# One transformer block in FP32 on one core: values get a buffer of their own, and the order of the stages is rewritten

## The reference

```python
x = x + attn_block(layernorm(x))     # pre-norm, LINEAR attention over the 16 heads of EACH token, MLP 256-1024-256
x = x + moe(layernorm(x))            # 8 experts, gates from the mean over the 2048 tokens of a batch

# attn_block, per token n (H=16 heads, HD=16):
fq, fk = elu(q) + 1, elu(k) + 1
kv = einsum('bhnd,bhne->bnde', fk, v);  qkv = einsum('bhnd,bnde->bhne', fq, kv)
attn = qkv / (einsum('bhnd,bnd->bhn', fq, fk.sum(1))[..., None] + 1e-6)
x = q_x + attn @ wo + bo
return x + (gelu(ln(x) @ fc_w + fc_b) @ proj_w + proj_b)

# moe: softmax over the logits that reach the second largest (normally 2 experts)
out = sum_e gates[b, e] * gelu(x @ expert_w[e].T + expert_b[e])
```

## Time and profile before

| | us |
|---|---|
| median of 3 runs | 1278.87 |
| the profiled execution | 1278.0 |
| its span on the core | 1276.2 |
| PE busy | 1108.7 (87% of the span) |
| DVE busy | 782.9 (61%) |
| ACT busy | 530.4 (42%) |
| POOL busy | 190.8 (15%) |
| one step, 9 to 10 (from the transposes of `X` to the next ones) | 68.55 |

### The profile page before, as it was taken

How to read it: one execution, slowest core, us unless ns; L and a number is a source line. 1 busy time by engine, 2 the same in 40 slices (tenths; PEclk the granted TensorE clock), 3 DMA queues, 4 the chain that set the end, 5 groups by cost and what they waited for, 6 DMA issues and landing times.

```text
span 1276.2 us, 22032 instructions
## 1 busy us (share of the span) xinstructions
PE 1108.7 (87%) x7272; PEld 816.2 (64%) x7272; DVE 782.9 (61%) x1692; ACT 530.4 (42%) x835; POOL 190.8 (15%) x113
## 2 busy tenths in 40 slices
PE   6646988979797989999997989999999989795946
PEld 3444766757575858686775758586767667583723
DVE  2465566565757586666756676766666674646333
ACT  2413443534444444536353454536363444231322
POOL 1011202020111212120301112121203012111000
PEclk9757897979797989989897989899897989797969
DMA  4966656383737475665737473656658374311013
GB/s 161 187 143 157 116 140 149 104 180 95 173 98 173 104 165 115 173 148 153 168 121 173 114 172 116 160 128 173 148 147 174 125 165 106 102 55 53 17 66 116
DMA packets 242518, 170.21 MB, mean 133 GB/s; under 512 B 177040, under 2 KB 218256, under 8 KB 240144
## 3 DMA queue, kind: packets, MB, share of 16 engines
q1 hardware_dynamic: 235792, 158.80, 52.3%
q10 hardware_dynamic: 6656, 10.50, 2.4%
HBM read 93.75 MB, written 75.50 MB: 133 GB/s over the span
## 4 chain that ended last, share of the span: by engine, by line
PE 48%; issue 23%; DVE 14%; ACT 7%; DMA 3%; SPq 2%; POOL 1%; DVEq 1%; ACTq 0%; POOLq 0%
PE pq L963 13%; PE pj L949 10%; PE ps L925 7%; PE pq L869 5%; PE pt L934 4%; PE pt L857 3%; DVE nd L727 2%; DVE acc L818 2%; DVE am L700 1%; DVE hn L631 1%; ACT am L513 1%; DVE stat L621 1%; DMA scratch_nd<-ot 1%; DMA ot<-scratch_v 1%; SPq L366 1%
## 5 line engine op out<-in xcount | busy, mean ns | idle before, releaser
L716 DVE TENSOR_TENSOR hidden<-xhT,hidden 128x512 fp32r<-128x512 f32 x128 | 96.6, 755 | 224.0 <-ACT hidden L541 224.0
L963 PE MATMUL pq<-hT,w_fc 128*128 128x512 f32 x768 | 225.4, 433 | 9.4 <-DVE hT L723 5.2
L540 ACT ACTIVATE xhT<-pq,col 128x512 f32<-128x512 f32 x128 | 88.0, 688 | 323.1 <-PE pq L963 322.9
L949 PE MATMUL pj<-w_pj,hidden 128*128 128x256 f32 x1536 | 214.1, 288 | 0.7 <-DVE hidden L716 0.7
L949 PEld LDWEIGHTS pj<-w_pj,hidden 128*128 128x128 f32 x1536 | 191.6, 189 | 18.6 <-issue 9.8
L925 PE MATMUL ps<-kq 48*128 48x128 f32 x1024 | 155.7, 436 | 24.0 <-DVE am L700 14.7
L963 PEld LDWEIGHTS pq<-hT,w_fc 128*128 128x128 f32 x768 | 149.0, 207 | 41.3 <-issue 7.7
L700 DVE TENSOR_TENSOR am<-ps,mask 128x512 f32<-128x512 f32 x256 | 164.1, 682 | 17.4 <-PE ps L925 17.1
L925 PEld LDWEIGHTS ps<-kq 48*128 48x128 f32 x1024 | 133.8, 329 | 61.1 <-issue 36.9
L869 PE MATMUL pq<-zT,w_e 128*128 (+1 forms) x256 | 119.4, 614 | 11.8 <-DMA b_e<-in_eb 7.3
L458 POOL TENSOR_TENSOR rs<-var,mhalf 128x4 f32<-128x4 f32 x16 | 18.1, 1132 | 571.2 <-DVE var L744 571.2
(11 more groups left out here) (117 smaller groups left out, 1399.3 us busy)
## 6 DMA issues: line engine op xcount, KB each, us to landing
kq<-scratch_q SPq DMA_DIRECT2D x192, 128.0 KB, 3.7
kq<-scratch_k SPq DMA_DIRECT2D x192, 128.0 KB, 4.5
scratch_q<-hidden SPq DMA_DIRECT2D x32, 512.0 KB, 4.6
scratch_k<-hidden SPq DMA_DIRECT2D x32, 512.0 KB, 6.1
scratch_nd<-ot SPq DMA_DIRECT2D x16, 1024.0 KB, 3.9
nd<-scratch_nd SPq DMA_DIRECT2D x48, 256.0 KB, 3.3
x_sb<-in_x SPq DMA_DIRECT2D x16, 512.0 KB, 4.7
scratch_v<-feat_v ACTq DMA_DIRECT2D x16, 512.0 KB, 2.8
```

Source lines behind the costliest of these rows:

```text
L540: nc.scalar.activation(gelub[:, u], pq[u][:, :], ACT.Gelu, bias=b_fc[:, m:m + 1])
L716: nc.vector.tensor_tensor(hidden[:, m % SLOTS, 1], gelub[:, u], hidden[:, m % SLOTS, 0].bitcast(f32), ALU.subtract).then_inc(S["rest_ready ...
L949: last = nc.tensor.matmul(pj[u][:, D * s:D * (s + 1)], hidden[:, m % SLOTS, a, lo:lo + P], w_pj[:, b, m], start=False, stop=end)
L963: last = nc.tensor.matmul(pq[m % 2][:, :], w_fc[:, b, c, P * m:P * (m + 1)], hT[:, a, c], start=(n == 0), stop=(n == len(order) - 1))
```

## The change

It does the following.

- The values get memory of their own, `vd`, as 128 partitions instead of 64. `VL` moves from behind `M4` to behind `M1`, and waits for the last `VT` instead of for the store of `ot`. `VT` moves from between `A2` and `F2` to ahead of `N`. It makes 8 transposes of 128 by 128.
- In `FULL`, `J7` comes ahead of `E`, `JA` directly behind `J7`, and `N` ahead of `F1`. In `HEAD`, `JA` also comes behind `J7` (and so ahead of `G`), and `F1` goes behind `A2` and `R`.
- `R` comes directly behind `A2`. The second expert's DVE part becomes a stage of its own, `F4`, behind `H`. `F2` is last in the list, and uses the banks `pj` in place of `pt`.
- The zero matmuls of L943 are gone: the first `down` matmul starts the accumulation.
- The ring of `x2_sb` shrinks from 2 to 1.

```diff
-X2RING = 2
+X2RING = 1
-FULL = ["L", "XS", "M1", "K0", "J2", "Y", "M2", "DS", "M3", "Z", "D1", "M4", "VL", "XL", "X", "E", "J7", "F1", "N", "D2", "K1", "A2", "F3",
-        "FX", "R", "VT", "F2", "B0", "H", "B9", "JA"]
-HEAD = ["L", "XS", "M1", "K0", "J2", "Y", "M2", "DS", "M3", "Z", "D1", "M4", "VL", "XL", "E", "X", "J7", "G", "N", "D2", "K1", "F1", "A2",
-        "F3", "FX", "R", "VT", "F2", "B0", "H", "B9", "JA"]
+FULL = ["L", "XS", "M1", "VL", "K0", "J2", "Y", "M2", "DS", "M3", "Z", "D1", "M4", "XL", "X", "J7", "JA", "E", "VT", "N", "F1", "D2", "K1", "A2",
+        "R", "F3", "B0", "H", "F4", "FX", "B9", "F2"]
+HEAD = ["L", "XS", "M1", "VL", "K0", "J2", "Y", "M2", "DS", "M3", "Z", "D1", "M4", "XL", "E", "X", "J7", "JA", "G", "VT", "N", "D2", "K1", "A2",
+        "R", "F1", "F3", "B0", "H", "F4", "FX", "B9", "F2"]
...
+        vd = sb("vd", [P, H * HALF])
-        vd = ot
...
                 if p.stage == "VL":
                     wait("v_out", at("v_out"))
-                    wait("nd_out", at("nd_out"))
+                    for u in range(2):
+                        wait(f"pt_full{u}", at(f"pt_full{u}"))
...
-                            sp.dma_start(vd[j:NQ * HD:NQ, H // 2 * b:H // 2 * (b + 1)], src[j, b]).then_inc(S["v_in"], 16)
+                            sp.dma_start(vd[2 * j + b::2 * NQ].rearrange("p (h t) -> p h t", h=H), src[j, b]).then_inc(S["v_in"], 16)
...
-                if p.stage == "F3":
+                if p.stage == "F4":
                     for m in range(NC):
-                        wait(f"pq_free{m}", at(f"pq_free{m}", 1))
+                        wait(f"pq_free{m}", at(f"pq_free{m}"))
...
                 if p.stage == "D2":
-                    copied(0)
+                    for c in range(NC):
+                        wait(f"pt_free{c}", features_copied[c])
...
                 if p.stage == "VT":
...
-                        for g in range(HG):
-                            group = rows[:, P * HG * u + g:P * HG * (u + 1):HG]
-                            last = nc.tensor.transpose(pt[u][:, n * g:n * (g + 1)], group, ident[0:n, 0:n])
+                        for g in range(HG // 2):
+                            last = nc.tensor.transpose(pt[u][:, P * g:P * (g + 1)], vd[:, HG // 2 * u + g::HG], ident[:, :])
...
                         if m == 0:
                             wait(f"pj_free{u}", at(f"pj_free{u}"))
-                            nc.tensor.matmul(pj[u][:, :], zero[:, :], zero[:, :].unsqueeze(1).broadcast_to([1, 4, P]), start=True, stop=False)
...
-                                                        start=False, stop=end)
+                                                        start=(m == 0 and n == 0 and s == 0), stop=end)
...
                 if p.stage == "F2":
                     wait("acc_ready", at("acc_ready"))
                     for u in range(2):
-                        wait(f"pt_free{u}", at(f"pt_free{u}"))
+                        wait(f"pj_free{u}", at(f"pj_free{u}"))
...
-                                last = nc.tensor.transpose(pt[u][:, D * s + P * m:D * s + P * (m + 1)],
+                                last = nc.tensor.transpose(pj[u][:, D * s + P * m:D * s + P * (m + 1)],
```

More of the change, by code:

```diff
@@ L74 @@
 INC = {
[L75 to L78, removed]
+    "pt_full0": {"W1": 1, "WS": 1, "X": 1, "D2": 1, "VT": 1, "H": 1, "G": 1},
+    "pt_free0": {"W1": 1, "WS": 1, "X": 1, "D2": 1, "VT": 1, "H": 1, "G": 1, **rounds("pt_free0")},
+    "pt_full1": {"X": 1, "D2": 1, "VT": 1, "H": 1},
+    "pt_free1": {"X": 1, "D2": 1, "VT": 1, "H": 1, **rounds("pt_free1")},
     "pq_full0": {"D2": 1, "F1": 1, "F3": 1, **rounds("pq_full0")},
@@ L87 @@
     "ps_free1": {"B0": 1, "B9": 1, "D2": 1, "A2": 1, "E": 1, **rounds("ps_free1")},
-    "pj_full0": {"J7": 1}, "pj_free0": {"JA": 1}, "pj_full1": {"J7": 1}, "pj_free1": {"JA": 1},
+    "pj_full0": {"J7": 1, "F2": 1}, "pj_free0": {"JA": 1, "F2": 1}, "pj_full1": {"J7": 1, "F2": 1}, "pj_free1": {"JA": 1, "F2": 1},
     "x_in": {"L": 16},
@@ L102 @@
     "pool_ready": {"G": 1}, "logit_ready": {"G": 1}, "gexp_ready": {"G": 1}, "gate_ready": {"G": 1},
-    "acc_ready": {"P": 1, "F1": 2, "F3": 2},
+    "acc_ready": {"P": 1, "F1": 2, "F4": 2},
     "out_stored": {"P": 16, "F2": 16},
@@ L161, in walk @@
     late = ["XS", "J2", "Z", "E"]
-    last = ["XL", "F1", "F3", "FX", "F2"]
+    last = ["XL", "F1", "F3", "F4", "FX", "F2"]
     def without(names, *out):
@@ L184, in walk @@
     stages(without(FULL, *first, *second), 17, [])
-    stages(["XS", "C1", "J2", "C2", "Z", "C3", "C4", "XL", "J7", "E", "F1", "F3", "FX", "F2", "JA"], 18, [])
-    stages(["XS", "J2", "Z", "XL", "E", "G", "F1", "F3", "FX", "F2"], 19, [])
+    stages(["XS", "C1", "J2", "C2", "Z", "C3", "C4", "XL", "J7", "JA", "E", "F1", "F3", "F4", "FX", "F2"], 18, [])
+    stages(["XS", "J2", "Z", "XL", "E", "G", "F1", "F3", "F4", "FX", "F2"], 19, [])
     loop(20, 23, last)
@@ L407, in run @@
                     for u in range(2):
-                        wait(f"pt_free{u}", at(f"pt_free{u}", 1))
+                        wait(f"pj_free{u}", at(f"pj_free{u}", 1))
                     sp.dma_start(out_t[p.t], out_sb[:, :, :]).then_inc(S["out_stored"], 16)
@@ L418, in _ @@
             nc.gpsimd.memset(mhalf[:, :], -0.5).then_inc(const_done, 1)
-            nc.gpsimd.memset(vd[:, :, :], 0.0).then_inc(const_done, 1)
+            nc.gpsimd.memset(vd[:, :], 0.0).then_inc(const_done, 1)
             nc.gpsimd.memset(vb[:, :, :], 1.0).then_inc(const_done, 1)
@@ L832, in run @@
                     for u in range(2):
-                        wait(f"pt_full{u}", at(f"pt_full{u}", 1))
+                        wait(f"pj_full{u}", at(f"pj_full{u}", 1))
                         o = out_sb[:, 2 * u:2 * u + 2]
-                        nc.vector.tensor_tensor(o, pt[u][:, :].rearrange("p (s d) -> p s d", d=D), o,
-                                                ALU.add).then_inc(S[f"pt_free{u}"], 1)
+                        nc.vector.tensor_tensor(o, pj[u][:, :].rearrange("p (s d) -> p s d", d=D), o,
+                                                ALU.add).then_inc(S[f"pj_free{u}"], 1)
             walk(dve, run)
@@ L845, in _ @@
                 pe.wait_ge(w_in[n], 16)
+            features_copied = []
             def run(p):
@@ L896, in run @@
                     transposes(xhat)
+                    features_copied[:] = [at(f"pt_free{c}", 1) for c in range(NC)]
                 if p.stage == "D2":
-                    copied(0)
+                    for c in range(NC):
+                        wait(f"pt_free{c}", features_copied[c])
                     for j in (4, 5, 0, 1, 2, 3):
@@ L1051, in run @@
                                 lo = P * (2 * u + s)
-                                last = nc.tensor.transpose(pt[u][:, D * s + P * m:D * s + P * (m + 1)],
+                                last = nc.tensor.transpose(pj[u][:, D * s + P * m:D * s + P * (m + 1)],
                                                            acc[:, m, lo:lo + P], ident[:, :])
-                        last.then_inc(S[f"pt_full{u}"], 1)
+                        last.then_inc(S[f"pj_full{u}"], 1)
             walk(pe, run)
```

10 lines of the change are left out of this document (4 added, 6 removed).

## The result

| | before | after |
|---|---|---|
| median | 1278.88 us (1278.82 to 1279.81) | 1310.76 us (1308.97 to 1314.52) |
| the profiled execution | 1278.0 | 1309.61 |
| its span | 1276.2 | 1307.8 |

The ratio after to before is 1.0257, with a 95% interval of 1.0232 to 1.0282. The kernel became 32 us slower. 1319 was forecast, with a range of 1290 to 1333.

What follows compares the result with a forecast made beforehand. PE was taken as near its bound but not on it, so order counts where PE waits. `FULL` steps +41, `HEAD` +3, the rest −4: +40 on 1278.0 us, the median 0.9 above, 1319 us; range 1290 to 1333.

Steps and rivals of the forecast that it cites:

- The hold on ACT: `FULL` steps, D2: ACT's write of `feat_v` waits for F1's products, now behind N; splits end 4.3 us later.
- The tail: `FULL` steps, A2 to M1: R directly behind A2, F4 and F2 ahead of `up`; with the later splits, `up` +6.8 us.
- The clock: M1 in `FULL` steps: PE's longer light stretch keeps the clock low, 0 to 3 us a step, 0.6 taken.
- Rival 3: M1 in `FULL` steps: clock stays low throughout, +2.5 us more a step, 1334 us; chance 0.10 together with rival 4.
- The zeros: Zero matmuls on PE: removing the pair brings back 0.53 us, on a PE without gaps.
- VT on PE: `FULL` steps: halving VT's transposes and moving them ahead of F1 count as nothing; 1 us a step if PE were the bound.
- HEAD: Steps 7, 11 and 15: tail +0.7 us, JA ahead of G and F1's products moved +0.3; +3 in all.
- Steps 2 to 6: N starts earlier without VL's loads, −2.5 us in all; zeros bring −0.5 each in steps 3 to 6.
- One sign of being wrong: The prediction counts as wrong if steps 3 to 6 change by more than 2 us.
- rival 1: `FULL` steps: only the tail is late, the hold on ACT costs nothing; +1.8 us a step, 1289 us; chance 0.12.
- rival 2: X to `up`: PE is the bound, less PE work in 16 tiles makes it faster, −24 us, 1255; chance 0.10.
- Rival 4: Part of the order doesn't act, such as an unseen hold on ACT: more, not less; chance 0.10 together with rival 3.

## Why the prediction was right, and where its sizes were off

**The hold on ACT was right.** Forecast: splits end at X+25.0; measured X+24.4, before X+20.7. The wait for `feat_v`, the 0.88 us of products and the 7.88 us from the first exp to the last split are there as worked out (0.95 us of products had been forecast). The mis-sized term is N's start: 6.38 us after its loads were taken, 5.65 were measured, and every later time down to F2's transposes is early by 0.6 to 0.7. I had called the full distance in step 17 typical; in step 5 it was 5.83 before and is 4.97 now, without VL's loads beside them.

**The tail was right.** R ends 7.96 us after the A2 additions start (7.95 forecast), the split 3.32 us after H starts, then F4, then F2. The transposes took 1.62 us to the next work instead of 1.89. That makes `up` early by 0.9: it came at X+38.98 (X+39.9 forecast). Over the six steps the stretch from X to `up` cost 35.8 us instead of 40.8.

**The clock went the other way.** I had charged 0.6 a step for a longer low clock in M1, and taken 0.5 for the zeros. From `up` to the first `down` the six steps won 4.4 us in all, where +0.6 was forecast; 2.1 of it in step 14, which in the kernel before had 10.37 us there against 8.23 now. In the other five it is 2.2 us, where the zeros alone make 2.65, so a longer low clock cost under 0.1 a step. Rival 3, the low clock through M1, is wrong: 0.92 is granted from 627 to 630, which begins 3.5 us behind the start of `up`, and 0.90 was from 617 to 620 before, 2.4 us behind it.

**The zeros were wrong in the end, right where they stood.** Their 0.53 us went out ahead of the first `down`, and from there to the next X 0.44 to 0.66 came back in four of the six steps, +2.4 in all, because the split now meets POOL's addition. The prediction's "on a PE without gaps" overlooked that the gap was missing only because of an accident of timing. That VT on PE counts as nothing was right for the changed kernel: A2's matmuls end at 605.45, and DVE comes to them at 608.80. Once ACT isn't held, the same place costs 0.9 us a `FULL` step, as the run with the values alone showed.

**HEAD.** +1 each forecast, +3.0 and −0.1 measured. JA ahead of G delays G's matmuls on PE: they start 4.15 us behind X instead of 2.31. PE in step 7 (X at 435.37) and, behind the dots, in step 11 (739.29) of the changed kernel:

```profile
439.52 0.81 PE L1022 MATMUL pt<-w_g,pb 128*128 128x8 f32 x4 [1.68 <-DVE pb L775]
440.72 1.97 PE L916 MATMUL pt<-ident,vd 128*128 128x128 f32 x8 [0.39 <-DVE held_at L780]
442.48 5.65 PE L908 MATMUL pq<-xhT,w_qkv 128*128 128x512 f32 x8
...
743.44 0.61 PE L1022 MATMUL pt<-w_g,pb 128*128 128x8 f32 x4 [1.69 <-DVE pb L775]
...
745.42 3.60 PE L908 MATMUL pq<-xhT,w_qkv 128*128 128x512 f32 x8
```

The same wait stands in both steps. In step 7 the work behind it ran partly at the low clock (5.65 us for 8 matmuls against 3.60), in step 11 not; the matmuls that follow these come 3.0 us later behind X in step 7. That is the difference of 3 us, and no row says why it fell only once.

**Steps 2 to 6** gained 6.1 instead of 4.5, and not as forecast: from X to `up`, where N's earlier start was to bring 2.5, they gained 1.1; from `up` to the first `down` 4.0, of which the zeros are 2.7; from there to the next X 1.0. One sign of being wrong, a change of more than 2 us in steps 3 to 6, did appear: step 6 alone gained 2.39. 1.5 of them lie behind the first `down`, where the granted clock was 0.79 before (412 to 420) and 1.00 now (407 to 415): that is the clock, for which the forecast had no term in these steps.

**The rivals.** Rivals 1 and 2 fell: with the hold alone the kernel before loses 17.9 us (rival 1 had it at nothing), and next to none of PE's gain reached the end (rival 2). Rival 4 had more than 1319. Terms in all: 33.9 for 41, 2.9 for 2, −6.1 for −4.5, the rest +0.9 for +1.7: 31.6 for 40.

**What I overlooked was in my own rows.** R's 3.39 us beside POOL stood in the sum as a fact. I didn't ask what it would be without POOL; that question was worth more than the whole change.

## What to carry to other kernels

When a list is reordered, follow each buffer that two stages share: here one `wait` on a reused buffer turned a harmless exchange of two names into 18 us. Before you move work on a busy engine, compare equal instructions on VectorE: if the same one takes 0.69 us here and 1.9 there, look at what GpSimd does at that moment, and move GpSimd's instruction if it has slack, to where VectorE works on PSUM. An instruction taken out of a full engine brings its time only if the next engine in the round isn't held by something that stays where it was.

## What the runs showed of the hardware

**A GpSimd addition holds up VectorE, and the other way round.** In every trace here that has the addition elsewhere, R's four `TENSOR_SCALAR` of 128x256 in FP32 take 1.38 to 1.39 us; they take 2.26 or 3.39 beside POOL's addition of 128x1024; a split of 128x512 takes 0.69 without and 1.27 to 1.97 beside it in the rows here. Whenever they began, R ended 1.12 us (1.11 to 1.13 in all 16 steps of the changed kernel) and the split 0.55 us behind POOL's end. POOL itself takes 2.34 us where it came first. In the kernel before it came while VectorE's F3 additions ran (605.73, 1.54 us), and took 2.82:

```profile
606.66 2.82 POOL L463 TENSOR_TENSOR x_sb<-x_sb,x 128x1024 f32 x1
```

VectorE's mask (L701, one input in PSUM) kept its 0.68 us within POOL's addition at 638.77. The Trainium skill, SBUF — State Buffer, "Who interferes with whom", says that VectorE and GpSimd share one port pair as an exclusive lock, held for the whole instruction by whoever issues first; that two inputs in SBUF, the on-chip memory beside PSUM, bring a VectorE instruction into it against a GpSimd one that reads there, and at most one doesn't, outside certain fast modes, which `TENSOR_SCALAR` can enter. The traces agree in each of these cases; whether R ran in such a mode no row shows.

**The same work isn't given the same clock.** In the kernel before, `up` starts at X+33.13 in step 9 and at X+33.23 in step 14, and from there to the first `down` it takes 8.39 and 10.37 us. In step 14 the granted clock stood at 0.50 until 976, 9.4 us behind the start of `up`. Why it rose later there no run here tells. The rule of the Trainium skill, TensorE: Matmul & The Clock Gate, Part 4 (PE-mode transpose), that transposes don't count as busy work in the same way, on which rival 3 leaned, was not tested: no run took the transposes ahead of `up` away and left the idle time.
